# Masked multiplies, the first layer norms and the low query weights move from VectorE to GpSimd, and two weight loads trade places

## The chip, the cores and the metric

One core of one Trainium2 chip runs the whole kernel in a single launch. The metric is device time in microseconds (us) for one execution. The engines are TensorE (PE in the profile, PEld its weight loads), VectorE (DVE), ScalarE (ACT), GpSimd (POOL) and SyncE (SP), which only issues transfers here. The program is written with explicit semaphores: each engine runs its own list of instructions in order.

## The reference, cut to what matters

Two blocks of gated cross attention and feed-forward over x (8 batches of 512 tokens, width 512) with a context of 8 x 120 rows.

```python
x = x + tanh(g_xattn[0]) * L0_xattn(_layernorm(x), ctx, ctx, W_q, W_k, W_v, W_o)      # 16 heads, no mask
x = x + tanh(g_ffn[0])   * L0_ffn(_layernorm(x), ...)                                  # experts
x = x + tanh(g_xattn[1]) * L1_xattn(_layernorm(x), ctx, ctx, mask, Wq, bq, Wk, bk, Wv, bv, Wo, bo)
x = x + tanh(g_ffn[1])   * L1_ffn(_layernorm(x), W_r, W_k, W_v, mu_r, mu_k)
# in L1_xattn:
scores = jnp.where(mask == 0, -1e30, scores)     # mask: key_mask (B, 120), the same for all heads
```

Every product is taken in float32 by three passes over a high and a low part of each operand (high times high, low times high, high times low). The kernel treats the mask of layer 1 in the keys: masked columns of the context are replaced, per batch, by the mean of the columns kept.

## The kernel before

The program has a keys-and-values phase (`keys_and_values`), then attention of layer 0 (`attention(..., 0)`), the experts, attention of layer 1, and the last feed-forward. The change touches only the first phase and the hand-over to the second.

The keys-and-values phase is a list of 32 units `n`: units 0 to 7 are the keys of layer 0, 8 to 15 its values, 16 to 23 the values of layer 1, 24 to 31 its keys. Each unit is 12 matmuls (`three_passes`, L154 to L156) into one of four PSUM banks, `n % 4`; a bank is free once the unit four before it has been evicted. Evictions: keys by ACT (high part, L315) and then DVE (low part, L384 or L381); values of layer 0 by ACT (L311); values of layer 1 by DVE (L389 and L390), with a bias row that ACT makes (L304, `bvm`). SP stores each result (L214, L215, L220), and an eviction into a staging buffer waits for the store that last read it.

Each of the five engines walks through the same 32 units, and tables of `{unit: what}` say behind which unit side work stands in that engine's queue. The side work on DVE is this:

- low parts of a weight (`SPLITS`, L333), from high parts that ACT copies when the weight has landed;
- the mask tables (`MASKS`, unit 6: `held`, `dropped`, `share`), then context times `held` (`KEPT`, L394), sums by batch (`MEANS`, L398, L401), and `fill = dropped * mean`, `craw += fill` (`FILLS`, L408, L410), all on 128 x 960 tiles; at unit 23 (`RENEW`) ACT and DVE make the new high and low parts (L323, L422), which the keys of layer 1 need;
- `norm(j)` at units 1, 5, ..., 29: mean and variance of batch j of x (L355, L359, L363, L364); POOL then takes the power (L281) and SP stores it;
- `first_norm(0)` at units 16 and 18 (`NORMED`) and `first_norm(1)` at 27 and 29: the transposed x of batch 0 and 1, minus the mean and times the reciprocal deviation (L785, L788; four instructions of each for a batch); ACT then copies the high parts (`NORMED_HIGH`, for batch 1 at unit 30), DVE the low ones (`NORMED_LOW`);
- the low parts of the query weights and the expert weights at unit 21 (`query_weights_low`, L776 and L765);
- from unit 23, for the first batch of attention: low queries (L1227) and row maxima of the scores (L1234).

PE does the queries of that batch behind units 23, 24 and 26 (it waits for the low query weights at 23) and its maximum tiles behind units 24 to 31 (L1437). Behind unit 31 it transposes the maxima (L1446) and begins the scores (L1465). POOL writes constant tables behind units 0, 2, 5, 8 and 11, and takes the powers. Weights k0 and k1 share slot 2 before: k1 is loaded at unit 8, v1 early into slot 0.

Of the kernel before, what the change touches and what calls it, by code (L numbers as in the profile page):

```python
# [20 lines left out]
ALU = mybir.AluOpType  # L21
ACT = mybir.ActivationFunctionType
AX = mybir.AxisListType
# [4 lines left out]
P = 128  # L28
B, T, D = 8, 512, 512
# [19 lines left out]
def f(ap):  # L49

    return ap.bitcast(F32)
# [25 lines left out]
QUERIES_AFTER = {23: (0, 1), 24: (2,), 26: (3,)}  # L77
MAXIMA_AFTER = {n: ((n - 24) // 2, (0, 1) if n % 2 == 0 else (2, 3)) for n in range(24, 32)}
MERGE_AT, NORM_AT, QUERIES_AT, MAXIMA_AT, ROWS_AT = 39, 40, (42, 44, 47, 51), (45, 49, 53, 55), 57
Ahead = namedtuple("Ahead", "load_weights load_first load_keys load_second load_output_weight constants first_norm query_weights_high query_weights_low first_norm_high "  # L80
                            "first_norm_low begin_act begin_dve begin_pe")

Begun = namedtuple("Begun", "load_ahead gather evict_act evict_dve on_act chosen")
# [77 lines left out]
def keys_and_values(nc, sb, sem, bank, ctx_t, weights, biases, mask, mask_t, x, kh_d, kl_d, v_d, norms_d, following):  # L161
# [6 lines left out]
    raw = [sb.over(f"kv_raw{i}", [P, C, D], f"kv_wl{i}") for i in range(3)]  # L168
    ch, cl, craw = sb("kv_ch", [P, C, N], F32R), sb("kv_cl", [P, C, N], F32R), sb("kv_craw", [P, C, N])
    held, dropped = sb("kv_held", [P, N]), sb("kv_dropped", [P, N])  # L170
    fill = held
    kh, kl = sb("kv_kh", [P, NK, HALF], F32R), sb("kv_kl", [P, NK, HALF], F32R)
    vo, bvm = sb("kv_vo", [S2, NV, D + 1]), sb("kv_bvm", [S2, 2, D])
    bk, bv = sb("kv_bk", [P, C]), sb("kv_bv", [S2, D])
# [9 lines left out]
    k_hi, k_lo, v_done = sem("kv_k_hi"), sem("kv_k_lo"), sem("kv_v_done")  # L184
    k_st, v_st = [sem(f"kv_k_st{i}") for i in range(NK)], [sem(f"kv_v_st{i}") for i in range(NV)]
    mask_in, held_done, vm_done, bvm_done = sem("kv_mask_in"), sem("kv_held_done"), sem("kv_vm_done"), sem("kv_bvm_done")
    filled, new_hi, new_lo = (sem("kv_" + s) for s in ("filled", "new_hi", "new_lo"))
    x_in, norm_st = [sem(f"kv_x_in{i}") for i in range(NX)], [sem(f"kv_norm_st{i}") for i in range(3)]
    const, ve_done, rstd_done = (sem("kv_" + s) for s in ("const", "ve_done", "rstd_done"))
    chain, pchain = sem("kv_chain"), sem("kv_pchain")  # L190

    units = [(lay, kind, u) for lay, kind in ((0, "k"), (0, "v"), (1, "v"), (1, "k")) for u in range(8)]
    SLOT, TURN_OF = (2, 1, 2, 0), (0, 2, 4, 3)
    SPLITS, MASKS = {3: 1, 10: 3, 20: 2}, 6
    KEPT, MEANS, FILLS, RENEW = {7: (0, 1), 8: (2, 3)}, {9: (0, 1), 11: (2, 3)}, {12: 0, 13: 1, 14: 2, 15: 3}, 23
    NORMED, NORMED_HIGH, NORMED_LOW = {16: (0, 1), 18: (2, 3)}, {18: (0, 1), 19: (2, 3)}, {19: (0, 1), 20: (2, 3)}
    QUERY_WEIGHT, QUERY_WEIGHT_LOW = 18, 21

    def sync(sp):
        def load_w(i):  # L200
            sp.dma_start(raw[SLOT[i]][:, :, :], weights[i].rearrange("(c p) n -> p c n", p=P)).then_inc(w_in[i], 16)
# [27 lines left out]
        load_x(1)  # L229
        sp.dma_start(bk[:, :], biases[0]).then_inc(bias_in, 16)  # L230
        sp.dma_start(bv[:, :], biases[1].partition_broadcast(S2)).then_inc(bias_in, 16)
        load_w(3)
        for n, (lay, kind, u) in enumerate(units):
            if n == 8:
                for b in range(NB):
                    sp.wait_ge(full[b], 2)
                load_w(2)
            if kind == "v":
                store_v(lay, u)
            else:  # L240
                store_k(lay, u)
            if n and n % 4 == 0:
                store_norm(n // 4 - 1)
            if n % 4 == 2 and n // 4 + NX < B:
                sp.wait_ge(ve_done, n // 4 + 1)
                load_x(n // 4 + NX)
            if n == 9:
                sp.wait_ge(norm_st[0], 16)
                sp.wait_ge(held_done, 1)
                following.load_first(sp)  # L250
            if n == 12:
                following.load_weights(sp)
            if n == 17:
                for b in range(NK):
                    sp.wait_ge(k_st[b], 32 * len(range(b, 8, NK)))
                sp.wait_ge(v_st[0], 16)
                following.load_keys(sp)
            if n == 23:
                sp.wait_ge(norm_st[1], 16)
                following.load_second(sp)  # L260
# [9 lines left out]
    def gpsimd(pool):  # L270
        steps = Steps(pool, pchain)
        pool.memset(mhalf[:, :], -0.5)
        steps.link(pool.memset(vo[:, :, D:D + 1], 1.0))
        pool.drain().then_inc(const, 1)

        for n in range(len(units)):
            following.constants(pool, n)
            if n % 4 == 1:
                j = n // 4
                pool.wait_ge(ve_done, j + 1)  # L280
                pool.tensor_tensor(norms[:, j, 1, :], ve[:, :], mhalf[:, :], ALU.pow).then_inc(rstd_done, 1)  # L281

    def scalar(act):
        def high_parts(i):
# [40 lines left out]

    def vector(dve):
        steps = Steps(dve, chain)

        def low_parts(hi, lo, whole, count):

            for c in range(C):
                dve.wait_ge(hi_done, count + c + 1)
                dve.tensor_tensor(lo[:, c], whole[:, c], f(hi[:, c]), ALU.subtract).then_inc(lo_done, 1)  # L333
# [29 lines left out]
            dve.tensor_scalar(norms[:, j, 0, :], mv[:, :, 0], 1.0, None, ALU.mult)  # L363
            dve.tensor_scalar(ve[:, :], mv[:, :, 1], EPS, None, ALU.add).then_inc(ve_done, 1)  # L364

        low_parts(wh[SLOT[0]], wl[SLOT[0]], raw[SLOT[0]], 0)
        low_parts(ch, cl, craw, C)
        for n, (lay, kind, u) in enumerate(units):
            k = (8 * lay + u) % (NK if kind == "k" else NV)
# [15 lines left out]
            elif lay:  # L385
# [3 lines left out]
                dve.tensor_scalar(vo[:, k, D:D + 1], vm[:, u:u + 1], 1.0, None, ALU.mult)  # L389
                dve.scalar_tensor_tensor(out=vo[:, k, 0:D], in0=src[0:S2, :], scalar=vm[:, u:u + 1],  # L390
                                         in1=bvm[:, u % 2, :], op0=ALU.mult, op1=ALU.add).then_inc(v_done, 1)
            if n in KEPT:
                for c in KEPT[n]:
                    ins = dve.tensor_tensor(craw[:, c], craw[:, c], held[:, :], ALU.mult)  # L394
                steps.link(ins)
            if n in MEANS:
                for c in MEANS[n]:
                    ins = dve.tensor_reduce(mean[:, c], craw[:, c].rearrange("p (b s) -> p b s", s=S2), AX.X, ALU.add)  # L398
                steps.link(ins)
                of = slice(MEANS[n][0], MEANS[n][-1] + 1)  # L400
                steps.link(dve.tensor_tensor(mean[:, of], mean[:, of],  # L401
                                             share[:, :].unsqueeze(1).broadcast_to([P, len(MEANS[n]), B]), ALU.mult))
            if n in FILLS:
                c = FILLS[n]
                by_batch = lambda a: a.rearrange("p (b s) -> p b s", s=S2)
                if c:
                    dve.wait_ge(filled, c)
                steps.link(dve.tensor_tensor(by_batch(fill[:, :]), by_batch(dropped[:, :]),  # L408
                                             mean[:, c].unsqueeze(2).broadcast_to([P, B, S2]), ALU.mult))
                dve.tensor_tensor(craw[:, c], craw[:, c], fill[:, :], ALU.add).then_inc(filled, 1)  # L410
            if n in NORMED:
                following.first_norm(dve, 0, NORMED[n])
            if n in NORMED_LOW:
                following.first_norm_low(dve, 0, NORMED_LOW[n])
            if n == QUERY_WEIGHT_LOW:
                following.query_weights_low(dve)
            if n % 4 == 1:
                norm(n // 4)
            if n == RENEW:
# [91 lines left out]
def attention(nc, lay, io, early, late, sem, eight, after, front=None, turned_place=None):  # L511
# [174 lines left out]
    def constants(pool, n):  # L686
# [30 lines left out]
        if n == 11:  # L717
            steps.link(pool.memset(pick[:, :, :, :], 0.0))
            for d in range(2):
                steps.link(pool.affine_select(out=pick[:, :, :, :], in_=pick[:, :, :, :],  # L720
                                              compare_op=ALU.not_equal, fill=1.0, base=-d,
                                              pattern=[[-2, C], [-8, C], [1, DK]], channel_multiplier=0))
            pool.drain().then_inc(const, 1)
        assert steps.n == (CONST_STEPS[n][1] - (merge and n == 0) if n in CONST_STEPS else 0)

    def spread_tables(pool):
# [27 lines left out]
    def query_weights_high(act):  # L754
# [3 lines left out]
        if route:  # L758
            act.wait_ge(w_in[2], 16)
            act.activation(wch[:, :, :], raw_c[:, :, :], ACT.Copy).then_inc(e_hi, 1)  # L760

    def query_weights_low(dve):
        low_parts(dve, 0)
        dve.wait_ge(e_hi, 1)
        dve.tensor_tensor(wcl[:, :, :], raw_c[:, :, :], f(wch[:, :, :]), ALU.subtract).then_inc(e_lo, 1)  # L765

    def output_weights_high(act):
        act.wait_ge(w_in[1], 16)
# [178 lines left out]
    def gpsimd(pool):  # L947
        if merge:
            constants(pool, 0)
        else:  # L950
            low_parts(pool, 1)

        def power(count):
# [213 lines left out]
    def vector(dve, step_of=None):  # L1167
# [69 lines left out]
        def begin(dve, n):  # L1237

            if n == 22:
                steps = Steps(dve, dchain)  # L1240
                dve.wait_ge(const, 1)
                steps.link(dve.tensor_reduce(part[:, :], ident[:, :].rearrange("p (a b) -> p b a", b=2)[:, 1, :], AX.X,
                                             ALU.add))
                steps.link(dve.tensor_scalar(part[:, :], part[:, :], -1.0, None, ALU.mult))
                dve.wait_ge(c_in, 16 * 4)
                dve.wait_ge(gated, 1)
            if n in (27, 29):
                first_norm(dve, 1, (n - 27, n - 26))
            if n in MAXIMA_AFTER:
                maxima(None, *MAXIMA_AFTER[n])  # L1250
            if n in QUERIES_AFTER:
                queries(0, QUERIES_AFTER[n])
# [426 lines left out]
    if merge:  # L1679
        return Engines(sync, gpsimd, scalar, vector, tensor), banks_free, ident, mhalf, \  # L1680
            Behind(load_behind, lambda act, k: scalar(act, k), lambda dve, k: vector(dve, k),
                   lambda pe, k: tensor(pe, None, k))
    ahead = Ahead(load_weights, load_first, load_first_keys, load_second, load_output_weight, constants, first_norm, query_weights_high, query_weights_low,
                  first_norm_high, first_norm_low,
                  lambda act, n: scalar(act, n), lambda dve, n: vector(dve, n), lambda pe, n: tensor(pe, None, n))
    return Engines(sync, gpsimd, scalar, vector, tensor), ahead
# [733 lines left out]
```

## Time and profile before

| | before |
|---|---|
| median of 3 runs | 1452.23 us (1450.77 to 1454.85) |
| the profiled execution's own time | 1454.85 us |
| its span, first to last instruction | 1453.1 us |
| mean granted TensorE clock | 0.965 of full speed |
| PE busy | 1311.5 us, 90% |
| DVE busy | 907.8 us, 62% |
| ACT busy | 571.1 us, 39% |
| POOL busy | 433.1 us, 30% |

How to read it: a busy share is a mean over the whole span and the phase at hand takes a tenth of it. So tables by stretch of time are of more use. A time in the trace counts from the span's start. An instruction's duration runs from its start to its end, and the next on the same engine may start slightly before that; where several alike stand in a row, the distance of their starts is their price. In brackets behind a row is the idle time of the engine before it, and what released it.

### The profile page before, as it was taken

What the parts mean: (1) busy time and instruction counts of PE and PEld (TensorE: products, weight loads), DVE (VectorE), ACT (ScalarE), POOL (GpSimd) and SP (SyncE); (2) the same over time, 40 slices, a digit from 0 to 9 for tenths busy, and PEclk for the clock granted to TensorE, in tenths of its full rate; (3) what the DMA queues carried; (4) which work ended last, traced back from release to release, by engine and by line L of the source; (5) the groups of instructions that cost most, each with busy time, mean ns of one, the idle gap of its engine ahead of it and who ended that gap; (6) DMA issues with size and microseconds to landing.
All of it is one profiled execution on the core that took longest, in us unless ns stands there. A gap on an engine that the chain in (4) does not pass through costs nothing.

```text
span 1453.1 us, 28305 instructions
## 1 busy us (share of the span) xinstructions
PE 1311.5 (90%) x10624; PEld 938.6 (65%) x10624; DVE 907.8 (62%) x1583; ACT 571.1 (39%) x1025; POOL 433.1 (30%) x351
## 2 busy tenths in 40 slices
PE   6976899999999979886989999999996789999997
PEld 5755567777777667622436666765764677777776
DVE  6986266656666546554546655656663577777762
ACT  3331444344434445443452342343243433333331
POOL 4300335432541100000442321331130644444450
PEclk9988899999999999988999999999998899999999
DMA  9862441444233556999883552462302311111100
GB/s 330 284 181 85 165 142 65 126 165 157 78 94 122 189 169 200 339 390 368 318 333 109 173 167 77 158 201 100 125 25 88 116 44 59 59 59 59 59 32 35
DMA packets 128852, 219.55 MB, mean 151 GB/s; under 512 B 27286, under 2 KB 48278, under 8 KB 124686
## 3 DMA queue, kind: packets, MB, share of 16 engines
q1 hardware_dynamic: 128782, 218.58, 44.2%
q8 instruction: 49, 0.80, 0.2%
q14 instruction: 21, 0.17, 0.0%
HBM read 135.67 MB, written 82.88 MB: 150 GB/s over the span
## 4 chain that ended last, share of the span: by engine, by line
PE 47%; issue 22%; DVE 13%; ACT 6%; POOL 5%; DMA 5%; SPq 2%; POOLq 0%; DVEq 0%; ACTq 0%
PE b L154 8%; PE b L156 7%; PE b L155 7%; PE b L1465 3%; PE b L1919 3%; PE b L1641 3%; DVE f_mix L2134 3%; PE b L1643 2%; PE b L1642 2%; PE b L1952 2%; PE b L1437 2%; PE b L1562 2%; POOL a_atl L997 2%; PE b L1571 2%; ACT e_gt L1838 2%
## 5 line engine op out<-in xcount | busy, mean ns | idle before, releaser
L1068 ACT ACTIVATE a_pr<-b 120x512 f32<-120x512 f32 x256 | 133.9, 603 | 126.3 <-PE b L1465 126.3
L1234 DVE TENSOR_REDUCE a_mx<-b 128x4 f32<-128x480 f32 x256 | 151.9, 652 | 4.6 <-PE b L1437 4.5
L997 POOL TENSOR_TENSOR a_atl<-a_pvs,a_ath 128x512 fp32r<-128x512 f32 x64 | 81.1, 1291 | 195.6 <-ACT a_ath L1114 195.6
L956 POOL TENSOR_TENSOR a_rstd<-a_ve,a_mhalf 128x4 f32<-128x4 f32 x16 | 16.2, 1012 | 319.1 <-DVE a_ve L1183 319.1
L154 PE MATMUL b<-a_xth,a_wqh 128*128 128x512 f32 x256 | 104.0, 406 | 5.6 <-DVE a_wql L776 5.6
L1641 PE MATMUL b<-a_woh,a_ath 128*128 128x512 f32 x256 | 105.2, 411 | 2.5 <-POOL a_atl L997 2.4
L1437 PE MATMUL b<-a_kbd,a_qh 128*128 128x480 f32 x256 | 86.9, 400 | 21.1 <-DVE a_mx L1234 20.7
L1643 PE MATMUL b<-a_woh,a_atl 128*128 128x512 f32 x256 | 101.7, 397 | 0.0
L155 PE MATMUL b<-a_xtl,a_wqh 128*128 128x512 f32 x256 | 101.7, 397 | 0.0
L1642 PE MATMUL b<-a_wol,a_ath 128*128 128x512 f32 x256 | 101.6, 397 | 0.0
L156 PE MATMUL b<-a_xth,a_wql 128*128 128x512 f32 x256 | 101.6, 397 | 0.0
L1363 DVE SCALAR_TENSOR_TENSOR a_x<-b,a_gate,a_x 128x512 f32 (+1 forms) x64 | 47.8, 747 | 83.5 <-PE b L1643 83.5
L2134 DVE SCALAR_TENSOR_TENSOR f_mix<-f_dif,f_mu,f_xt 128x512 f32<-128x512 f32 x64 | 69.8, 1109 | 27.9 <-PE b L156 12.5
L1437 PEld LDWEIGHTS b<-a_kbd,a_qh 128*128 128x128 f32 x256 | 47.9, 190 | 43.6 <-DVE a_mx L1234 25.7
L1571 PE MATMUL b<-a_pr,a_vals 120*32 120x512 f32 x512 | 67.8, 600 | 0.0
L1838 ACT ACTIVATE e_gt<-b 128x512 f32<-128x512 f32 x87 | 46.1, 602 | 53.2 <-PE b L1919 53.2
L154 PEld LDWEIGHTS b<-a_xth,a_wqh 128*128 128x128 f32 x256 | 48.5, 189 | 26.2 <-issue 10.0
L2096 POOL TENSOR_TENSOR f_xmkl<-f_mix,f_xmkh 128x512 fp32r<-128x512 f32 x32 | 48.5, 1529 | 51.4 <-ACT f_xmkh L2108 51.4
L1641 PEld LDWEIGHTS b<-a_woh,a_ath 128*128 128x128 f32 x256 | 48.7, 190 | 18.3 <-issue 8.0
L1224 DVE SCALAR_TENSOR_TENSOR a_ql<-b,a_bq,a_qh 128x512 fp32r<-128x512 f32 x32 | 24.0, 751 | 56.9 <-ACT a_qh L1029 56.9
L2201 ACT ACTIVATE f_ka<-b 128x512 f32<-128x512 f32 x32 | 19.1, 597 | 98.4 <-PE b L156 92.9
L1952 PE MATMUL b<-e_gt,e_inner 32*64 32x512 f32 x384 | 51.3, 649 | 7.0 <-ACT e_xc L1856 3.3
(221 smaller groups left out, 3231.0 us busy)
## 6 DMA issues: line engine op xcount, KB each, us to landing
a_rp<-s_rp SPq DMA_DIRECT2D x128, 256.0 KB, 4.5
s_x<-a_x SPq DMA_DIRECT2D x16, 1024.0 KB, 4.2
s_rp<-e_chosen SPq DMA_DIRECT2D x16, 1024.0 KB, 7.7
s_rp<-e_xc SPq DMA_DIRECT2D x16, 1024.0 KB, 7.7
kv_xb<-in_x SPq DMA_DIRECT2D x8, 1024.0 KB, 8.3
a_xr<-in_x_t SPq DMA_DIRECT2D x8, 1024.0 KB, 6.6
a_x<-in_x SPq DMA_DIRECT2D x8, 1024.0 KB, 7.9
s_xn<-a_xn SPq DMA_DIRECT2D x8, 1024.0 KB, 4.8
```

The costliest lines, as they stand in the source:

```text
L154: pe.matmul(out, ah, bh, start=(c == 0), stop=False)
L155: pe.matmul(out, ah, bl, start=False, stop=False)
L156: last = pe.matmul(out, al, bh, start=False, stop=(c == C - 1))
L997: pool.tensor_tensor(atl[:, g], pvs[:, g], f(ath[:, g]), ALU.subtract).then_inc(a_lo, 1)
L1068: act.activation(pr[:, h % RING, :], bank[k][0:S2, :], ACT.Exp, scale=SCALE)\
L1234: dve.tensor_reduce(mx[:, t, :, r], bank[k][:, 0:HJ * S2].rearrange("p (a s) -> p a s", a=HJ), AX.X, ALU.max).then_inc(free[k], 1)
L1437: pe.matmul(bank[k][:, 0:HJ * S2], qh[:, r, t * P:(t + 1) * P], kbd[:, r, :], start=True, stop=True)\
L1571: ins = pe.matmul(bank["v"][a * DK:(a + 1) * DK, :], v[:, h * DK:(h + 1) * DK], pr[:, h % RING, :], start=True, stop=True)
L1641: pe.matmul(out, ath[:, m, cols], woh[:, m, :], start=(m == 0), stop=False)
L1642: pe.matmul(out, ath[:, m, cols], wol[:, m, :], start=False, stop=False)
L1643: ins = pe.matmul(out, atl[:, m, cols], woh[:, m, :], start=False, stop=(m == C - 1))
L2134: dve.scalar_tensor_tensor(out=mix[:, a, c % 2], in0=dif[:, c], scalar=mu[:, a, c:c + 1], in1=xt[:, c, 0:T], op0=ALU.mult, op1=ALU.add).th ...
```

## The change

- The slots of the weights: k0 and v1 now share slot 0 and k1 has slot 2. SP loads k1 early and v1 at unit 8, the other way about than before. The low parts of v1 are made at unit 11 (10 before) and those of k1 at 19 (20 before).
- Context times `held` is done by POOL, one chunk at units 9, 10, 12 and 13; a semaphore `kept` tells DVE. The means are taken chunk by chunk at units 11, 12, 14 and 15.
- The fills stand at units 16 to 19 and are, for each chunk, eight `scalar_tensor_tensor` of 120 columns (one for each batch) instead of two instructions of 960.
- `first_norm(0)` is done by POOL at units 15 and 17, behind the power of unit 17; `first_norm(1)` by POOL after unit 31's turn of its loop. The copies of the high parts stand at 18 and 20 (batch 0) and, unchanged, at 30 (batch 1).
- The low parts of the query and expert weights are made by POOL at unit 19; ACT makes the high ones at 17 (18 before).

```diff
-    SLOT, TURN_OF = (2, 1, 2, 0), (0, 2, 4, 3)
-    SPLITS, MASKS = {3: 1, 10: 3, 20: 2}, 6
-    KEPT, MEANS, FILLS, RENEW = {7: (0, 1), 8: (2, 3)}, {9: (0, 1), 11: (2, 3)}, {12: 0, 13: 1, 14: 2, 15: 3}, 23
-    NORMED, NORMED_HIGH, NORMED_LOW = {16: (0, 1), 18: (2, 3)}, {18: (0, 1), 19: (2, 3)}, {19: (0, 1), 20: (2, 3)}
-    QUERY_WEIGHT, QUERY_WEIGHT_LOW = 18, 21
+    SLOT, TURN_OF = (0, 1, 2, 0), (0, 2, 4, 3)
+    SPLITS, MASKS = {3: 1, 11: 3, 19: 2}, 6
+    KEPT, MEANS, FILLS, RENEW = {9: 0, 10: 1, 12: 2, 13: 3}, {11: 0, 12: 1, 14: 2, 15: 3}, {16: 0, 17: 1, 18: 2, 19: 3}, 23
+    NORMED, NORMED_HIGH, NORMED_LOW = {15: (0, 1), 17: (2, 3)}, {18: (0, 1), 20: (2, 3)}, {20: (0, 1), 21: (2, 3)}
+    QUERY_WEIGHT = 17
...
-        load_w(3)
+        load_w(2)
         for n, (lay, kind, u) in enumerate(units):
             if n == 8:
                 for b in range(NB):
                     sp.wait_ge(full[b], 2)
-                load_w(2)
+                load_w(3)
...
         for n in range(len(units)):                      # gpsimd
             following.constants(pool, n)
+            if n in KEPT:
+                c = KEPT[n]
+                pool.wait_ge(held_done, 1)
+                pool.wait_ge(lo_done, C + c + 1)
+                pool.tensor_tensor(craw[:, c], craw[:, c], held[:, :], ALU.mult).then_inc(kept, 1)
             if n % 4 == 1:
                 j = n // 4
                 pool.wait_ge(ve_done, j + 1)
                 pool.tensor_tensor(norms[:, j, 1, :], ve[:, :], mhalf[:, :], ALU.pow).then_inc(rstd_done, 1)
+            if n in NORMED:
+                following.first_norm(pool, 0, NORMED[n])
...
             if n in MEANS:                               # vector
-                for c in MEANS[n]:
-                    ins = dve.tensor_reduce(mean[:, c], craw[:, c].rearrange("p (b s) -> p b s", s=S2), AX.X, ALU.add)
...
+                c = MEANS[n]
+                dve.wait_ge(kept, c + 1)
+                steps.link(dve.tensor_reduce(mean[:, c], craw[:, c].rearrange("p (b s) -> p b s", s=S2), AX.X, ALU.add))
+                steps.link(dve.tensor_tensor(mean[:, c], mean[:, c], share[:, :], ALU.mult))
             if n in FILLS:
                 c = FILLS[n]
-                steps.link(dve.tensor_tensor(by_batch(fill[:, :]), by_batch(dropped[:, :]),
-                                             mean[:, c].unsqueeze(2).broadcast_to([P, B, S2]), ALU.mult))
-                dve.tensor_tensor(craw[:, c], craw[:, c], fill[:, :], ALU.add).then_inc(filled, 1)
-            if n in NORMED:
-                following.first_norm(dve, 0, NORMED[n])
+                for b in range(B):
+                    ins = dve.scalar_tensor_tensor(out=craw[:, c, of_batch(b)], in0=dropped[:, of_batch(b)],
+                                                   scalar=mean[:, c, b:b + 1], in1=craw[:, c, of_batch(b)],
+                                                   op0=ALU.mult, op1=ALU.add)
+                ins.then_inc(filled, 1)
...
+        if route and n == 19:                            # constants(pool, n)
+            for c in range(C):
+                pool.wait_ge(w_hi[0], c + 1)
+                pool.tensor_tensor(wql[:, c], raw_q[:, c], f(wqh[:, c]), ALU.subtract).then_inc(w_lo[0], 1)
+            pool.wait_ge(e_hi, 1)
+            pool.tensor_tensor(wcl[:, :, :], raw_c[:, :, :], f(wch[:, :, :]), ALU.subtract).then_inc(e_lo, 1)
...
         else:                                            # attention's gpsimd, ahead of its first turn
+            first_norm(pool, 1, range(C))
             low_parts(pool, 1)
...
-            if n in (27, 29):                            # attention's begin(dve, n)
-                first_norm(dve, 1, (n - 27, n - 26))
```

## Rows read from the trace of the kernel before

**Rows 1.** The head of the profile's page.

```profile
span 1453.1 us, 28305 instructions
PE 1311.5 (90%) x10624; PEld 938.6 (65%) x10624; DVE 907.8 (62%) x1583; ACT 571.1 (39%) x1025; POOL 433.1 (30%) x351
```

**Rows 2.** Stretches: busy time (instructions) of each engine, granted clock, DMA share, GB/s.

```profile
40.00:60.00 20.00, 20.00 (x88) 15.63 (x87) 19.60 (x32) 5.49 (x10) 6.99 (x7) 1.00 1.02 323
60.00:80.00 20.00, 17.08 (x66) 12.76 (x65) 19.74 (x40) 7.18 (x12) 2.86 (x2) 0.91 0.76 231
80.00:100.00 20.00, 12.72 (x47) 9.21 (x46) 19.76 (x43) 10.89 (x17) 1.01 (x1) 0.83 0.54 142
```

**Rows 3.** PE in order of time (start, duration), and one stretch of 5 us.

```profile
91.01 0.80 PE L154 MATMUL b<-a_xth,a_wqh 128*128 128x512 f32 x1 [5.59 <-DVE a_wql L776]
...
125.46 0.77 PE L1437 MATMUL b<-a_kbd,a_qh 128*128 128x480 f32 x1 [3.12 <-DVE a_mx L1234]
...
139.36 1.33 PE L1437 MATMUL b<-a_kbd,a_qh 128*128 128x480 f32 x2 [6.08 <-DVE a_mx L1234]
...
125.00:130.00 5.00, 4.54 (x14) 3.70 (x15) 2.73 (x5) 0.00 (x0) 0.00 (x0) 0.66 0.28 99
```

**Rows 4.** DVE's groups, 0 to 150 us: busy us, mean ns | idle before.

```profile
L785 DVE TENSOR_TENSOR a_xr<-a_xr,a_mr 128x512 f32<-128x512 f32 x8 | 8.9, 1147 | 0.0
L788 DVE TENSOR_TENSOR a_xr<-a_xr,a_mr 128x512 f32<-128x512 f32 x8 | 8.6, 1109 | 0.0
...
L394 DVE TENSOR_TENSOR kv_craw<-kv_craw,kv_held 128x960 f32<-128x960 f32 x4 | 5.5, 1421 | 0.0
...
L408 DVE TENSOR_TENSOR kv_held<-kv_dropped,kv_mean 128x960 f32<-128x960 f32 x4 | 4.6, 1156 | 0.1
...
L422 DVE TENSOR_TENSOR kv_cl<-kv_craw,kv_ch 128x960 fp32r<-128x960 f32 x4 | 4.4, 1152 | 0.0
...
L776 DVE TENSOR_TENSOR a_wql<-a_raw_q,a_wqh 128x512 fp32r<-128x512 f32 x4 | 2.5, 689 | 0.0
```

**Rows 5.** POOL in order of time, and one of its groups over the whole span.

```profile
134.85 1.78 POOL L281 TENSOR_TENSOR kv_norms<-kv_ve,kv_mhalf 128x4 f32<-128x4 f32 x1 [21.53 <-DVE kv_ve L364]
163.29 4.98 POOL L776 TENSOR_TENSOR a_wol<-a_raw_o,a_woh 128x512 fp32r<-128x512 f32 x4 [26.67 <-ACT a_woh L770]
...
178.09 2.54 POOL L997 TENSOR_TENSOR a_atl<-a_pvs,a_ath 128x512 fp32r<-128x512 f32 x2 [0.57 <-ACT a_ath L1114]
180.58 6.45 POOL L785 TENSOR_TENSOR a_xr<-a_xr,a_mr 128x512 f32<-128x512 f32 x4
...
L968 POOL TENSOR_TENSOR a_sums<-a_pick,a_vals 120x512 f32<-120x512 f32 x8 | 8.3, 1040 | 18.2 <-DMA a_vals<-s_v 18.2
```

**Rows 6.** DVE and POOL in order of time while both run, 37 to 44 us.

```profile
37.68 0.62 POOL L713 TENSOR_SCALAR_AFFINE_SELECT a_xr<-a_xr 128x480 f32<-128x480 f32 x1
39.17 1.15 DVE L394 TENSOR_TENSOR kv_craw<-kv_craw,kv_held 128x960 f32<-128x960 f32 x1
39.20 1.59 POOL L713 TENSOR_SCALAR_AFFINE_SELECT a_xr<-a_xr 128x480 f32<-128x480 f32 x1
40.24 1.56 DVE L394 TENSOR_TENSOR kv_craw<-kv_craw,kv_held 128x960 f32<-128x960 f32 x1
40.93 1.33 POOL L713 TENSOR_SCALAR_AFFINE_SELECT a_xr<-a_xr 128x480 f32<-128x480 f32 x1
41.83 1.44 DVE L394 TENSOR_TENSOR kv_craw<-kv_craw,kv_held 128x960 f32<-128x960 f32 x1
42.33 1.39 POOL L715 CAST a_mpick<-a_xr 128x480 fp32r<-128x480 f32 x1
```

**Rows 7.** Line 1338 by itself (ns min/median/max), and both engines near its longest.

```profile
L1338 DVE SCALAR_TENSOR_TENSOR a_rx<-a_rx,a_part,a_rs x16: 350/350/1273, 169.7 to 1130.8; 128x128 fp32r<-128x128 f32 x16
...
1130.78 1.27 DVE L1338 SCALAR_TENSOR_TENSOR a_rx<-a_rx,a_part,a_rs 128x128 fp32r<-128x128 f32 x1
...
1128.86 3.04 POOL L2096 TENSOR_TENSOR f_xmkl<-f_mix,f_xmkh 128x512 fp32r<-128x512 f32 x2 [1.29 <-ACT f_xmkh L2108]
```

**Rows 8.** The load issued at 41.63 (last number: us to landing), and ACT's eviction of unit 15.

```profile
kv_raw<-in_k SPq DMA_DIRECT2D x1, 1024.0 KB, 8.5
...
63.05 0.60 ACT L311 ACTIVATE kv_vo<-b 120x512 f32<-120x512 f32 x1 [3.40 <-DMA s_v<-kv_vo]
```

**Rows 9.** DVE and PE in order of time: the last norm and the phase's end.

```profile
131.61 0.69 DVE L355 BATCH_NORM_STATS2 kv_stats<-kv_xb 128x6 f32<-128x512 f32 x1
...
134.61 0.16 DVE L364 TENSOR_SCALAR kv_ve<-kv_mv 128x4 f32<-128x4 f32 x1
...
148.32 0.63 PE L1446 MATMUL b<-a_ident,a_mx 128*128 128x128 f32 x4 [2.33 <-DVE a_mx L1234]
```

More of the change, by code:

```diff
@@ L79 @@
 MERGE_AT, NORM_AT, QUERIES_AT, MAXIMA_AT, ROWS_AT = 39, 40, (42, 44, 47, 51), (45, 49, 53, 55), 57
-Ahead = namedtuple("Ahead", "load_weights load_first load_keys load_second load_output_weight constants first_norm query_weights_high query_weights_low first_norm_high "
+Ahead = namedtuple("Ahead", "load_weights load_first load_keys load_second load_output_weight constants first_norm query_weights_high first_norm_high "
                             "first_norm_low begin_act begin_dve begin_pe")
@@ L170, in keys_and_values @@
     held, dropped = sb("kv_held", [P, N]), sb("kv_dropped", [P, N])
-    fill = held
     kh, kl = sb("kv_kh", [P, NK, HALF], F32R), sb("kv_kl", [P, NK, HALF], F32R)
@@ L186, in keys_and_values @@
     mask_in, held_done, vm_done, bvm_done = sem("kv_mask_in"), sem("kv_held_done"), sem("kv_vm_done"), sem("kv_bvm_done")
-    filled, new_hi, new_lo = (sem("kv_" + s) for s in ("filled", "new_hi", "new_lo"))
+    kept, filled, new_hi, new_lo = (sem("kv_" + s) for s in ("kept", "filled", "new_hi", "new_lo"))
     x_in, norm_st = [sem(f"kv_x_in{i}") for i in range(NX)], [sem(f"kv_norm_st{i}") for i in range(3)]
@@ L327, in vector @@
         steps = Steps(dve, chain)
+        of_batch = lambda b: slice(b * S2, (b + 1) * S2)
         def low_parts(hi, lo, whole, count):
@@ L364, in norm @@
             dve.tensor_scalar(ve[:, :], mv[:, :, 1], EPS, None, ALU.add).then_inc(ve_done, 1)
-        low_parts(wh[SLOT[0]], wl[SLOT[0]], raw[SLOT[0]], 0)
+        low_parts(wh[0], wl[0], raw[0], 0)
         low_parts(ch, cl, craw, C)
@@ L391, in vector @@
                                          in1=bvm[:, u % 2, :], op0=ALU.mult, op1=ALU.add).then_inc(v_done, 1)
[L392 to L395, printed above, removed]
             if n in MEANS:
-                for c in MEANS[n]:
-                    ins = dve.tensor_reduce(mean[:, c], craw[:, c].rearrange("p (b s) -> p b s", s=S2), AX.X, ALU.add)
[L399 to L402, printed above, removed]
+                c = MEANS[n]
+                dve.wait_ge(kept, c + 1)
+                steps.link(dve.tensor_reduce(mean[:, c], craw[:, c].rearrange("p (b s) -> p b s", s=S2), AX.X, ALU.add))
+                steps.link(dve.tensor_tensor(mean[:, c], mean[:, c], share[:, :], ALU.mult))
             if n in FILLS:
                 c = FILLS[n]
-                by_batch = lambda a: a.rearrange("p (b s) -> p b s", s=S2)
-                if c:
-                    dve.wait_ge(filled, c)
-                steps.link(dve.tensor_tensor(by_batch(fill[:, :]), by_batch(dropped[:, :]),
-                                             mean[:, c].unsqueeze(2).broadcast_to([P, B, S2]), ALU.mult))
-                dve.tensor_tensor(craw[:, c], craw[:, c], fill[:, :], ALU.add).then_inc(filled, 1)
-            if n in NORMED:
-                following.first_norm(dve, 0, NORMED[n])
+                for b in range(B):
[3 more added lines that the diff above has]
+                ins.then_inc(filled, 1)
             if n in NORMED_LOW:
                 following.first_norm_low(dve, 0, NORMED_LOW[n])
-            if n == QUERY_WEIGHT_LOW:
-                following.query_weights_low(dve)
             if n % 4 == 1:
@@ L760, in query_weights_high @@
             act.activation(wch[:, :, :], raw_c[:, :, :], ACT.Copy).then_inc(e_hi, 1)
[L762 to L765, printed above, removed]
     def output_weights_high(act):
@@ L1682, in attention @@
                    lambda pe, k: tensor(pe, None, k))
-    ahead = Ahead(load_weights, load_first, load_first_keys, load_second, load_output_weight, constants, first_norm, query_weights_high, query_weights_low,
+    ahead = Ahead(load_weights, load_first, load_first_keys, load_second, load_output_weight, constants, first_norm, query_weights_high,
                   first_norm_high, first_norm_low,
```

## The prediction

> **What bounds the kernel now.** I read the page's head first [rows 1], then the table of stretches [rows 2]. The diff reorders only the first tenth, the keys-and-values phase, so that is the place to look. From 40 to 100 us VectorE (DVE) is busy 19.6 to 19.8 of every 20 us while TensorE (PE) falls from 20.0 to 12.7: DVE sets the pace. After 100 us neither is full and they wait for each other. The reader sees this in PE's own rows [rows 3]: before the first query matmul it sat idle 5.59 us for the low weights that DVE writes; at 125.46 and 139.36 it waited 3.12 and 6.08 us for row maxima that stood in DVE's queue behind first_norm. The phase ends where PE turns the maxima, at 148.32; everything later hangs on that point.
>
> **The change: what leaves DVE.** Durations are from [rows 4] (a group's busy time). Between DVE's first masking multiply (39.17) and the end of its RENEW low parts (100.9, the 4.4 us group of L422) leave: the four masking multiplies 5.5; half of L785 and L788 (batch 0), 8.75; the low query weights 2.5 plus one more of that width, 0.6. The fills were 4.6 (L408) and as much again (L410), 9.2. They become 32 multiply-adds of 120 columns. No such row exists; 960 and 512 columns cost 1.09 and 0.62 each, so the slope gives 0.2 for 120; I take 0.18, 32 are 5.8, saving 3.4. (Bounds: 0.13 by columns alone, 0.35 by the lone 128-column row [rows 7].) Two more mean multiplies add 0.3. Sum taken off: 5.5 + 8.75 + 3.1 + 3.4 - 0.3 = 20.5.
>
> **What GpSimd (POOL) pays.** By [rows 5] first_norm costs 1.61 per instruction (6.45 for 4), a low part 1.25 to 1.27, a pow 1.0 undisturbed (1.78 at worst). A 960-column multiply isn't there: from 1.27 by columns 2.35; bounds 1.95 to 3.0 (from the plain 1.04 of a 512-column product elsewhere and from 1.61).
>
> **The two engines block each other.** The masking stretch shows it [rows 6]: POOL's L713 takes 0.62 alone, but 1.59 and 1.33 while DVE's two-input multiplies run, and DVE's 1.15 becomes 1.56 and 1.44. They take turns, one whole instruction each: DVE 40.24 can't read until POOL's ends, POOL's 40.93 until DVE's ends at 41.80, and DVE's 41.83 again waits. It hits small instructions hardest [rows 7]: a 128-column L1338 normally takes 0.35 and took 1.27, ending just after POOL's L2096. The Trainium skill (SBUF — State Buffer, Who interferes with whom) says the same in its own terms: a DVE instruction with two SBUF inputs and a GpSimd one that reads SBUF exclude each other for the whole instruction; the trace agrees, and this rule speaks against the change. Evictions from PSUM and bn_stats have at most one SBUF input; in 180 to 193 us POOL's rate stays 1.61 beside them.
>
> **Waits that come in, followed instruction by instruction.**
> 1. v1's weight is now the one loaded late, at unit 8, and needed at unit 11. Its predecessor in that place of the queue (issued 41.63) took 8.5 us [rows 8], so it lands at 50.1; ScalarE (ACT) copies until 50.8. DVE gets there at 39.2 + 3.1 for the norm [rows 9] = 42.3. POOL starts masking at 41.1 (43.7 in the trace, less 2.6 it lost to L394), and is at its third product until 51.65: mask, pow, mask, 2.4 of constants, mask. DVE waits 9.35.
> 2. The second low part waits for the fourth mask: 2.35.
> 3. Then two means, the norm until 62.1, pow until 63.1 and first_norm's first four. Two mean multiplies wait for it: 1.9. The eviction of unit 16 isn't the bound: it could begin once ACT has evicted unit 15 at 63.05, which waits for a store [rows 8].
> 4. Unit 16's fills meet the last two of those four: 0.9 + 1.6 = 2.5.
> 5. Unit 17's norm ends at 76.6 and releases POOL just as DVE goes into unit 18. POOL now has a pow, four first_norm and five low parts in a row. Each of the eight fills waits for one: 0.35 + 4 x 1.61 + 3 x 1.25 = 10.5. They end at 89.2.
> 6. The last two POOL low parts hold up k1's: 2.5.
>
> Sum 29.1. DVE ends RENEW 29.1 - 20.5 = 8.6 later, at 109.5. PE follows: unit 23 needs the eviction of unit 19, queued behind all of 5 and 6, at about 95, so the earlier weights (about 90) don't help it.
>
> **After RENEW.** Batch 1's first_norm leaves DVE. PE's wait of 3.12 and some slow clock after it go: in 125 to 130 us the granted clock is 0.66 [rows 3], that is 1.7 us. I take 4.8 in all, up to the last norm. The second half no longer matters to PE alone, since POOL runs all eight after that norm, ACT waits for them at unit 30, and unit 31's keys are behind it in ACT's queue. Before, from 134.77 to 148.32 took 13.55 [rows 9]. Now: pow 1.0 + 8 x 1.61 = 12.9 + ACT's last copy 0.63 and eviction 0.66 + DVE 0.72 and maxima 1.22 + hand-overs 0.4 = 17.5. That is +3.9. PE, DVE and SP's next loads wait with it; the output weights of the next turn follow on POOL but are not due for 15 us. The earlier k1 load and the turned inputs land well ahead and cost nothing; if v1's landed 3 us later, all would be 3 later.
>
> Total: +8.6 - 4.8 + 3.9 = +7.7. The profiled execution took 1454.85, 2.6 above the median of 1452.2; the difference applies to either, so I forecast 1452.2 + 7.7 = 1459.9, about 1460.
>
> **Rivals.**
> - *Relief wins (faster).* The small fills slip past POOL, several or all between two of its instructions, because a 0.13 us read may find the port free. Then waits 3 to 6 (17.4) go; PE is bound by POOL's low query weights at about 84.5 instead. Queries end at 91.7 and unit 24 at 94.4 against 102.1: -7.7, then -4.8 + 3.9: -8.6, 1443.6. For it: no row has several tiny DVE instructions against a POOL run. Against: [rows 6, 7]. It decides when the six waits together fall under 21.6.
> - *It cancels.* A few fills pass per gap, so wait 5 is 3.5 rather than 10.5: +0.7, 1453. For: the gaps of POOL are unknown; against: in [rows 6] DVE's next instruction never got in ahead of a waiting POOL.
> - *The early stretch hurts more.* Masks of 3.0: +2.6, and v1 landing later: 1463. [Rows 5] speak for the smaller figure.
>
> **Chances.** Forecast with its own spread (masks 1.95 to 3.0: -1.5 to +2.6; fills clear of POOL: -0.8 to +2.6; clock 1 either way) 1456.5 to 1464: 0.55, and the heavier early stretch 0.1. Relief 0.18, cancelling 0.17. No change means within 0.3%, 4.4 us, about what this kernel's measurement can tell. The forecast lies 3.3 beyond that bound; of its 0.65, 0.05 falls inside. So slower 0.6, same 0.22, faster 0.18. The likeliest case's range is 1456.5 to 1464; as both signs are alive, the range given is 1444 to 1464.
>
> **What the next profile will show.** Right: DVE idle from about 42 to 51 in front of wl; the new 120-column fills, of which eight lie about 1.3 to 1.8 apart around 78 to 89; PE with one gap of over 10 us before unit 23; ACT waiting for POOL's mult before unit 31's keys; PE's transposed maxima near 156. Wrong: fills evenly 0.2 apart beside a busy POOL (then faster); v1's weight landing before 46; POOL's first_norm over 2 us apiece; the transposed maxima under 145.

## The result

| | before | changed |
|---|---|---|
| median | 1453.14 us (1450.77 to 1454.85, 4 runs) | 1462.16 us (1461.76 to 1464.07, 4 runs) |
| span of the profiled execution | 1453.1 us | 1461.7 us |

Changed over before is 1.0065, 95% interval 1.0048 to 1.0084: slower by 9.0 us (7 to 12). 1460 had been forecast, in a range of 1444 to 1464 (from a base of 1452.2, the median before a fourth run of before had joined).

First the head of the profile's page after the change. DVE is busy only 7 us less than before [rows 1] and POOL 37 us more.

```profile
PE 1308.4 (90%) x10624; PEld 937.8 (64%) x10624; DVE 900.5 (62%) x1584; ACT 571.1 (39%) x1025; POOL 470.0 (32%) x376
```

The stretches, against [rows 2]. From 40 to 60 us DVE is down from 19.60 to 12.83, but that is no relief: 6.95 us of it are idling before v1's low parts (the next block), and what left its list there is made up by waits. From 80 to 100 us it is busy all 20.00, while PE has fallen from 12.72 to 8.76 and the granted clock from 0.83 to 0.63. A DVE instruction that waits for POOL counts as busy, as the next blocks show.

```profile
40.00:60.00 20.00, 20.00 (x88) 15.66 (x87) 12.83 (x21) 5.56 (x10) 13.49 (x10) 1.00 1.02 321
60.00:80.00 20.00, 15.37 (x62) 11.41 (x62) 19.71 (x51) 9.61 (x17) 10.17 (x7) 0.94 0.82 245
80.00:100.00 20.00, 8.76 (x27) 6.41 (x27) 20.00 (x30) 4.29 (x7) 11.84 (x9) 0.63 0.34 88
```

DVE in order of time, changed kernel (start, duration; in brackets the idle time before). The first row is v1's low parts, late behind the weight; then the same eight 120-column fills (L407) at four units; L340 at 87.31 is k1's low parts.

```profile
50.75 5.56 DVE L340 TENSOR_TENSOR kv_wl<-kv_raw,kv_wh 128x512 fp32r<-128x512 f32 x4 [6.95 <-ACT kv_wh L293]
...
67.38 4.21 DVE L407 SCALAR_TENSOR_TENSOR kv_craw<-kv_dropped,kv_mean,kv_craw 128x120 f32<-128x120 f32 x8
...
72.24 2.10 DVE L407 SCALAR_TENSOR_TENSOR kv_craw<-kv_dropped,kv_mean,kv_craw 128x120 f32<-128x120 f32 x8
...
78.07 9.32 DVE L407 SCALAR_TENSOR_TENSOR kv_craw<-kv_dropped,kv_mean,kv_craw 128x120 f32<-128x120 f32 x8
87.31 5.68 DVE L340 TENSOR_TENSOR kv_wl<-kv_raw,kv_wh 128x512 fp32r<-128x512 f32 x4
...
104.64 4.36 DVE L418 TENSOR_TENSOR kv_cl<-kv_craw,kv_ch 128x960 fp32r<-128x960 f32 x4
```

The last row is RENEW's low parts, which end at 109.0. In the kernel before they ended at 100.9:

```profile
96.53 4.36 DVE L422 TENSOR_TENSOR kv_cl<-kv_craw,kv_ch 128x960 fp32r<-128x960 f32 x4
```

The same eight fills take 2.10, 4.21 or 9.32 us. What POOL does at those times explains it: nothing at 72.24, the last two of a run of four at 67.38, and at 78.07 the beginning of a run of nine.

```profile
63.23 3.36 POOL L782 TENSOR_TENSOR a_xr<-a_xr,a_mr 128x512 f32<-128x512 f32 x2
66.56 3.37 POOL L785 TENSOR_TENSOR a_xr<-a_xr,a_mr 128x512 f32<-128x512 f32 x2
77.52 1.01 POOL L285 TENSOR_TENSOR kv_norms<-kv_ve,kv_mhalf 128x4 f32<-128x4 f32 x1 [7.59 <-DVE kv_ve L371]
78.49 3.11 POOL L782 TENSOR_TENSOR a_xr<-a_xr,a_mr 128x512 f32<-128x512 f32 x2
81.56 3.16 POOL L785 TENSOR_TENSOR a_xr<-a_xr,a_mr 128x512 f32<-128x512 f32 x2
84.69 5.49 POOL L723 TENSOR_TENSOR a_wql<-a_raw_q,a_wqh 128x512 fp32r<-128x512 f32 x4
90.14 1.71 POOL L725 TENSOR_TENSOR a_wcl<-a_raw_c,a_wch 128x512 fp32r<-128x512 f32 x1
```

And PE, the rows that answer to [rows 3] and the last of [rows 9]: one wait of 11.24 us before unit 23, and one of 11.72 at the end. Of the two waits for maxima in between, the one of 3.12 is gone and the one of 6.08 has shrunk to 2.11 (at 140.19).

```profile
93.86 0.75 PE L154 MATMUL b<-kv_wh,kv_ch 128*120 128x512 f32 x1 [11.24 <-DVE kv_vo L397]
...
156.03 1.09 PE L1442 MATMUL b<-a_ident,a_mx 128*128 128x128 f32 x4 [11.72 <-DVE a_mx L1232]
```

The transposed maxima come at 156.03 instead of 148.32, 7.7 later. The reader can find that gap in the chain of work that ended last: the last norm's power, then eight POOL instructions, then ACT's eviction of unit 31. PE's own last work ends at 144.31, and from there on it is idle.

```profile
139.66 1.01 POOL kv_norms L285
140.66 6.10 POOL a_xr L782 x4
146.77 5.91 POOL a_xr L785 x4
152.72 0.51 issue
153.23 0.65 ACT kv_kh L321
```

### The profile page after: what moved, and what is told of

Its sections match the earlier page's. It is cut to its first block, busy times and chain, and to the rows that moved or that the text cites. A ratio compares the mean times of both kernels' runs of the same rounds, so it can differ in the third digit from the quotient of the medians.

```text
span 1461.7 us, 28338 instructions
## 1 busy us (share of the span) xinstructions
PE 1308.4 (90%) x10624; PEld 937.8 (64%) x10624; DVE 900.5 (62%) x1584; ACT 571.1 (39%) x1025; POOL 470.0 (32%) x376
## 4 chain that ended last, share of the span: by engine, by line
PE 48%; issue 22%; DVE 12%; ACT 6%; POOL 5%; DMA 4%; SPq 1%; POOLq 0%; DVEq 0%; ACTq 0%
PE b L154 8%; PE b L156 8%; PE b L155 7%; PE b L1461 3%; PE b L1637 3%; PE b L1638 3%; PE b L1639 3%; PE b L1915 2%; DVE f_mix L2130 2%; PE b L1948 2%; PE b L1558 2%; PE b L1433 2%; ACT a_pr L1066 2%; POOL a_atl L995 2%; PE b L1567 2%
## 5 line engine op out<-in xcount | busy, mean ns | idle before, releaser
L1637 PE MATMUL b<-a_woh,a_ath 128*128 128x512 f32 x256 | 106.2, 415 | 3.6 <-POOL a_atl L995 3.6
L1637 PEld LDWEIGHTS b<-a_woh,a_ath 128*128 128x128 f32 x256 | 49.1, 192 | 19.2 <-issue 9.2
L1639 PEld LDWEIGHTS b<-a_woh,a_atl 128*128 128x128 f32 x256 | 49.4, 193 | 11.9
```

Of the source, the lines that this page charges most:

```text
L1637: pe.matmul(out, ath[:, m, cols], woh[:, m, :], start=(m == 0), stop=False)
L1639: ins = pe.matmul(out, atl[:, m, cols], woh[:, m, :], start=False, stop=(m == C - 1))
```

## The experiments

The yardstick beside the median is the start of the transposed maxima: 148.32 before, 156.03 changed. It comes from one profile each. It shows where in the phase a difference arises, which a median can't (single executions of before ran from 1448.98 to 1458.16 us; its medians beside the experiments were 1453.8, 1453.7 and 1454.1).

The mark carries the TensorE clock of that one execution, and this part can be read off. With first_norm(1) gone from DVE, PE waits for maxima twice, 2.11 us each (120.96 and 140.19 in the changed kernel), and runs the same matmuls between. From the end of one wait to the end of the other it takes 17.7 us in four profiles (wide fills, low parts back, first_norm(0) back, before with first_norm(1) at unit 25) and 19.2 in the five others, where one stretch of 5 us after the first wait was granted only 0.66 to 0.77. So 1.5 us between two marks can be the clock alone. What decides it isn't shown: the wait ahead of it is 2.11 or 2.12 us in all nine.

**Is work on POOL free for DVE?** Two kernels add useless work on POOL to the kernel before, once with reads, once without, on a spare tile that nothing else uses.

```diff
+    spare = sb("kv_spare", [P, D])                   # and a memset of it once, at the start
...
                 pool.tensor_tensor(norms[:, j, 1, :], ve[:, :], mhalf[:, :], ALU.pow).then_inc(rstd_done, 1)
+            if n == 17:
+                for _ in range(10):                   # second kernel: range(24)
+                    steps.link(pool.tensor_tensor(spare[:, :], spare[:, :], spare[:, :], ALU.mult))
+                                                      # second kernel: pool.memset(spare[:, :], 0.0)
```

> The kernel before, with ten more 512-column multiplies on POOL, both inputs and the output in a spare tile, right after the power of unit 17, about 77 to 90 us. They compute nothing that is used. Theory A: DVE, with two-input work in that stretch, waits for most of them, up to 1.27 us each: RENEW ends 7 to 12 us later, time 6 to 12 more. Rival (engines run beside each other freely): below 1 us.

> The kernel before, with 24 memsets of the same spare tile on POOL instead, 0.5 us each, so the same 12 us of POOL time at the same place without a read. Theory A (the two exclude each other only where POOL reads SBUF): within 1 us of the kernel before. If any POOL work slowed DVE: as much as with the multiplies.

With the multiplies: 1460.30 us, ratio 1.0052 (1.0036 to 1.0069), maxima at 154.31. With the memsets: 1455.22 us, 1.0015 (1.0005 to 1.0025), maxima at 148.72. k1's low parts (four of DVE's) and POOL beside them, first with the multiplies:

```profile
77.14 17.96 POOL L286 TENSOR_TENSOR kv_spare<-kv_spare 128x512 f32<-128x512 f32 x10
...
84.00 5.86 DVE L338 TENSOR_TENSOR kv_wl<-kv_raw,kv_wh 128x512 fp32r<-128x512 f32 x4
```

then with the memsets:

```profile
77.21 13.95 POOL L286 MEMSET kv_spare<- 128x512 f32 x24
...
83.01 2.49 DVE L338 TENSOR_TENSOR kv_wl<-kv_raw,kv_wh 128x512 fp32r<-128x512 f32 x4
```

5.86 against 2.49 for the same four. 14 us of POOL writes leave DVE's durations as they were. Beside POOL's multiplies seven of DVE's two-input instructions lost 0.84 us each and three more about 0.1; DVE had been 0.4 ahead, and RENEW ended 5.9 later, just under the 7 to 12 that I had expected. The 1.5 us that the memsets seem to cost is a little over the 1 us expected, and its interval (1.0005 to 1.0025) lies above 1. RENEW isn't later there (it begins at 96.13, before at 96.53), so up to there it doesn't come of DVE waiting; where it comes from isn't shown. So the price lies in the pairing of reads. The Trainium skill (SBUF — State Buffer, Who interferes with whom) makes just this distinction between a GpSimd instruction that reads SBUF and one that only writes; both runs agree.

**Is it the eight small fills?**

```diff
-                for b in range(B):
-                    ins = dve.scalar_tensor_tensor(out=craw[:, c, of_batch(b)], in0=dropped[:, of_batch(b)], ...)
-                ins.then_inc(filled, 1)
+                steps.link(dve.tensor_tensor(by_batch(held[:, :]), by_batch(dropped[:, :]), mean[:, c]..., ALU.mult))
+                dve.tensor_tensor(craw[:, c], craw[:, c], held[:, :], ALU.add).then_inc(filled, 1)
```

> The changed kernel with each fill as two 960-column instructions again (4 x 2 instead of 4 x 8). Theory A: the sum of both engines' work in the stretch counts, not the size of the pieces. Fills cost 9.3 instead of 8.3 by themselves, POOL's nine instructions stay: RENEW's low parts end within 2 us of 109.0, time within 2 us of the changed kernel's. Rival C (eight small fills, each behind one long POOL instruction, are the loss): two waits instead of six in unit 18, 5 us earlier or more.

1463.82 us, 1.0071 (1.0049 to 1.0092): no gain. RENEW ends at 108.0 against 109.0, and this execution was already 0.9 ahead at v1's low parts. (The maxima stand at 154.17, 1.9 earlier; 1.5 of that is the clock, this being one of the four profiles with 17.7.) The waits moved on to what follows:

```profile
79.15 2.54 DVE L411 TENSOR_TENSOR kv_craw<-kv_craw,kv_held 128x960 f32<-128x960 f32 x1
81.61 7.52 DVE L340 TENSOR_TENSOR kv_wl<-kv_raw,kv_wh 128x512 fp32r<-128x512 f32 x4
```

The fills end at 81.7 instead of 87.4, and k1's low parts take 7.52 instead of 5.68, then the next fills wait as well. As long as DVE's queue holds such work, it goes at POOL's pace, mostly one instruction of DVE's for each of POOL's, whichever instructions do the waiting. A turn lasts about as long as POOL's instruction, with DVE's own time inside it: in unit 18 a fill takes 1.59 to 1.68 us beside POOL's 1.56 to 1.64, and 1.34 beside 1.30. The rival of the small pieces falls.

**Is it the late load of v1?**

```diff
-    SLOT, TURN_OF = (0, 1, 2, 0), (0, 2, 4, 3)
+    SLOT, TURN_OF = (2, 1, 2, 0), (0, 2, 4, 3)        # v1 loaded early, k1 at unit 8, as before
```

> The changed kernel with the slots and the two weight loads back as before (v1 loaded early, k1 at unit 8), all else changed. Theory A (DVE and POOL take turns on two-input work, and the tail waits for POOL): the 7 us that DVE stands idle before v1's low parts go, but unit 16's eviction can't be earlier than about 64.6, when ACT has evicted unit 15 and made the bias row, and it stands at 66.7 now; so the transposed maxima come 1 to 3 us earlier than at 155.9. Rival B (the late load is the loss): 7 to 9 us earlier.

1463.20 us, 1.0065 (1.0049 to 1.0082), maxima at 154.75, 1.3 earlier. The 6.95 us of idling at 50.75 are gone, and most of them come back further on:

```profile
43.70 4.57 DVE L340 TENSOR_TENSOR kv_wl<-kv_raw,kv_wh 128x512 fp32r<-128x512 f32 x4
...
65.25 0.15 DVE L396 TENSOR_SCALAR kv_vo<-kv_vm 120x1 f32<-120x1 f32 x1 [6.03 <-ACT kv_bvm L310]
```

Unit 16's eviction waits for ACT, and ACT for a store of values (63.90 here, 63.05 in [rows 8]). So the late load is worth 1.4 us, not the 9 that DVE loses there.

**Which of the moved work pays?** Two kernels give part of it back to DVE.

```diff
+            if n == 21:                                # vector; taken from POOL's unit 19
+                following.query_weights_low(dve)
```

> The changed kernel with the five low parts of the query and expert weights on DVE at unit 21 again. Theory A: POOL's run behind unit 17 shrinks from nine to four instructions, 6.5 us less for DVE to wait, 3.1 more for it to do: RENEW ends 3 to 4 us earlier, time 3.4 less than the changed kernel's. If work on POOL were free for DVE, it would be 3 us later instead.

```diff
-            if n in NORMED:                            # gpsimd, NORMED = {15: (0, 1), 17: (2, 3)}
-                following.first_norm(pool, 0, NORMED[n])
+            if n in NORMED:                            # vector, NORMED = {16: (0, 1), 18: (2, 3)}
+                following.first_norm(dve, 0, NORMED[n])
```

> The changed kernel with first_norm(0) on DVE at units 16 and 18 again. Theory A: DVE has 8.75 us more to do, and loses about 10 us of waits (two mean multiplies 1.8, two fills 2.3, four fills 6.2); the five low parts of POOL at unit 19 still meet DVE's two-input work. RENEW ends between 3 us earlier and 1 us later. If POOL's work were free for DVE: 8 us later.

Low parts back: RENEW ends at 106.2 (2.8 earlier with 3.1 more work on DVE), maxima at 151.66, 4.4 earlier, of which 1.5 is the clock; 1461.28 us, 1.0055 (1.0038 to 1.0072), which the median alone doesn't tell from the changed kernel (3.4 less had been expected). first_norm(0) back: 8.3 us more work on DVE by its rows, and RENEW ends at 108.3, 0.7 earlier; maxima at 153.76, 2.3 earlier, again 1.5 of it the clock; 1463.31 us, 1.0069 (1.0052 to 1.0086). With the low parts back, POOL's run ends at 84.2 and k1's low parts are at their own price again:

```profile
77.42 7.44 DVE L407 SCALAR_TENSOR_TENSOR kv_craw<-kv_dropped,kv_mean,kv_craw 128x120 f32<-128x120 f32 x8
84.78 2.48 DVE L340 TENSOR_TENSOR kv_wl<-kv_raw,kv_wh 128x512 fp32r<-128x512 f32 x4
```

Neither move to POOL had relieved DVE: each costs it as much in waits as in work, or more.

**The tail.** First the changed kernel, then the kernel before, each with first_norm(1) at unit 25 of POOL's loop; then the kernel before with it where the change puts it.

```diff
+            if n == 25:                                # gpsimd, behind the power of unit 25
+                following.first_norm(pool, 1, range(C))
...
-            first_norm(pool, 1, range(C))              # ahead of attention's first turn (or DVE's units 27 and 29)
```

> The changed kernel with first_norm(1) on POOL right after the power of unit 25 instead of after unit 31's turn of its loop. Theory A: it lies at about 121 to 134, beside DVE work with at most one SBUF input, so it costs nothing; ACT evicts unit 31 when PE is done with it, near 142 instead of 153.2, and the transposed maxima come 9 to 12 us earlier, about 145.5; time about 1451.5. Rival D (the tail is not on the path; PE would be late anyway): under 3 us.

> The kernel before, with first_norm(1) alone moved to POOL, right after the power of unit 25. It stands beside DVE work with at most one SBUF input. Theory A: PE's waits of 3.12 and 6.08 us shrink by 3.1 and 4.0 and its clock has no such pauses to fall in; the transposed maxima come 8 to 11 us earlier than at 148.3; time 1442 to 1445. Rival (another wait takes over, such as ACT waiting for POOL at unit 30): under 4 us gained.

> The kernel before with first_norm(1) alone moved to POOL, after unit 31's turn of its loop as in the changed kernel. It puts the prediction's two last terms by themselves: -4.8 up to the last norm (its ve at about 130 instead of 134.6), +3.9 from there to the transposed maxima. Theory A: the maxima at 147.5, 0.9 earlier than before, so no change in time (within 2 us). Against the run with it at unit 25, whose maxima stand at 138.54, the same work is 9 us later for its place in POOL's queue alone.

| first_norm(1) | maxima at | median | over before |
|---|---|---|---|
| changed, after the loop | 156.03 | 1462.16 | 1.0065 (1.0048 to 1.0084) |
| changed, at unit 25 | 147.03 | 1452.20 | 0.9992 (0.9980 to 1.0004) |
| before + POOL after the loop | 148.11 | 1454.97 | 1.0009 (0.9995 to 1.0022) |
| before + POOL at unit 25 | 138.54 | 1443.46 | 0.9933 (0.9917 to 0.9950) |

The marks of the last three rows of the table, as the profiles have them:

```profile
147.03 0.63 PE L1443 MATMUL b<-a_ident,a_mx 128*128 128x128 f32 x4 [2.40 <-DVE a_mx L1233]
148.11 1.08 PE L1445 MATMUL b<-a_ident,a_mx 128*128 128x128 f32 x4 [11.79 <-DVE a_mx L1235]
138.54 0.93 PE L1446 MATMUL b<-a_ident,a_mx 128*128 128x128 f32 x4 [2.40 <-DVE a_mx L1236]
```

The same eight instructions, at a place where DVE has no work with two SBUF inputs and nobody yet waits, are worth 9.0 and 9.6 us of the mark (of the 9.6 the clock gave 1.5; the first pair has the same clock). That is twice: the whole loss of the change in one case, and a kernel 10 us faster than before in the other. Of the last kernel, POOL, then ACT:

```profile
113.22 6.51 POOL L787 TENSOR_TENSOR a_xr<-a_xr,a_mr 128x512 f32<-128x512 f32 x4
119.69 6.45 POOL L790 TENSOR_TENSOR a_xr<-a_xr,a_mr 128x512 f32<-128x512 f32 x4
129.95 1.01 POOL L281 TENSOR_TENSOR kv_norms<-kv_ve,kv_mhalf 128x4 f32<-128x4 f32 x1 [3.81 <-DVE kv_ve L366]
...
128.97 2.17 ACT L795 ACTIVATE a_xth<-a_xr 128x512 fp32r<-128x512 f32 x4
135.75 0.66 ACT L317 ACTIVATE kv_kh<-b,kv_bk 128x480 fp32r<-128x480 f32 x1 [4.60 <-PE b L156]
```

ACT's copies need no wait and its eviction of unit 31 waits for PE alone.

**A version with the masks as well**, on the best one: masks on POOL at units 9, 10, 12 and 13, small fills at 12 to 15.

```diff
-    KEPT, MEANS, FILLS = {7: (0, 1), 8: (2, 3)}, {9: (0, 1), 11: (2, 3)}, {12: 0, 13: 1, 14: 2, 15: 3}
+    KEPT, MEANS, FILLS = {9: 0, 10: 1, 12: 2, 13: 3}, {12: 0, 13: 1, 14: 2, 15: 3}, {12: 0, 13: 1, 14: 2, 15: 3}
```

> The kernel before with first_norm(1) on POOL at unit 25, and in addition the masking multiplies on POOL (units 9, 10, 12, 13) and small fills in place of wide ones, at units 12 to 15 as before, so that they end before anything else is on POOL. DVE saves 5.5 + 1; it can't evict unit 16 before about 64.6 (ACT evicts unit 15 at 63.05 and makes the bias row), against 67.6, so at most 3 us come of it; the low parts of v1 meet the masks and lose up to 2 each. Theory A: maxima at 135.5 to 138.5, time 1440.5 to 1443.5. If the masks' turns with DVE cost more than they save: later than 138.5.

Maxima at 141.51, 3.0 later than without the masks on POOL; 1444.36 us, 0.9936 (0.9913 to 0.9959), so the median sees no difference. I had expected 135.5 to 138.5. Half of the 3.0 is the clock (19.2 here, 17.7 there), the other half was there at the end of RENEW (102.4 against 100.8): the fills are dearer than I had them, and the first eight met two masks.

```profile
49.99 6.16 DVE L407 SCALAR_TENSOR_TENSOR kv_craw<-kv_dropped,kv_mean,kv_craw 128x120 f32<-128x120 f32 x8
```

## Why the prediction was right, step by step

- **DVE sets the pace up to RENEW; relief must be counted net of waits.** Right. RENEW ended at 109.0 (forecast 109.5) against 100.9.
- **What leaves DVE, 20.5.** Too high by 2.4 for the fills. Eight of them alone take 2.10 us, 0.26 each from start to start, not 0.18. The slope between wide instructions had given 0.2, and I had gone below it without a reason; 0.26 lies inside my bounds (0.13 to 0.35).
- **Wait 1, 9.35.** v1 landed 8.5 us after its issue, ACT was done as forecast: 6.95 of idling, 1.5 for the norm's L370 behind a mask (1.66 instead of 0.17; the prediction had that instruction free) and 1.0 in the first low part: 9.4. But its worth was only 1.4, as the run with the early load shows; about 2 us separated it from the next bound, ACT's eviction of unit 15, which the prediction named without drawing that conclusion.
- **Waits 2 to 4, 2.35, 1.9 and 2.5.** 2.1, 1.8 (L403 took 1.74 and 0.41 instead of 0.17) and 2.1.
- **Waits 5 and 6, 10.5 and 2.5.** 7.2 (9.32 less 2.10) and 3.2 (5.68 less 2.49). The turns are as foreseen, one fill for one POOL instruction, but two fills slipped by while POOL took the power, so the fills met six POOL instructions and not seven (1.6 with the power's rest). And a turn lasts as long as POOL's instruction with the fill's 0.26 inside, where I had added the two (another 1.6). Wait 5 was too long by 3.3, and that cancels the error of the fills: two wrong terms of opposite sign stand behind the good 8.6 (8.1 measured). That closeness is luck.
- **-4.8 up to the last norm.** 3.3: from RENEW's end the norm came 30.6 us later, before 33.9. PE's wait behind first_norm is gone, but the clock fell elsewhere, to the lower of its two levels (1.2 instead of 2.4 GHz) for part of a stretch: 120 to 125 us was granted 0.71 (first row), where before the same matmuls had 1.00 in 112 to 117 (second row). The term itself was right for a profile without that fall: in the kernel before the last norm came 4.9 earlier with first_norm(1) at unit 25 (17.7 us between the waits), and 3.15 earlier with it after the loop (19.2).

```profile
120.00:125.00 5.00, 3.96 (x10) 2.96 (x11) 3.19 (x9) 0.00 (x0) 1.01 (x1) 0.71 0.27 99
```

```profile
112.00:117.00 5.00, 4.07 (x17) 3.13 (x18) 3.11 (x7) 0.27 (x1) 1.01 (x1) 1.00 0.27 100
```

- **+3.9 in the tail.** 2.9: 16.45 us from the last norm to the maxima, before 13.55. POOL's eight took 12.1, not 12.9 (1.5 each).
- **Sum +7.7.** 8.1 - 3.3 + 2.9 = 7.7 at the maxima. But 1.5 of it is the clock of the one profiled execution, which no term held; without that fall it would be 6.2, so the exact match is chance. The medians differ by 9.0, the spans by 8.6. Up to 210 us the delay stays at 7.8 (POOL's next power begins at 209.53, before at 201.74); where the last us arises I haven't shown, and it is within the interval.
- **The rivals.** "Relief wins" needed small fills that pass POOL; the only two that did so stood beside a power. "It cancels" needed a gain of 7 in wait 5; it was 3.3. "The early stretch hurts more" needed masks of 3.0 or a later v1; the first took 2.26, and v1 came as forecast.

## What to carry to other kernels

Before moving elementwise work from VectorE to GpSimd, list what VectorE will be running at that moment. Against work with two SBUF inputs VectorE falls to GpSimd's slower pace, and in this case the move gained nothing. Against evictions from PSUM, reductions and the statistics instructions it was free, and 10 us were to be had that way here. And look who stands behind the new instruction: placed behind the last norm it kept ScalarE idle for 12 us, and the last eviction came 9 us later (153.23 instead of 144.24 with it at unit 25). A stall of 9 us may be worth 1.4 if another bound stands 2 us behind it.

## What I had not expected of the hardware

- "Two inputs" is not the whole of it. The norm's L370 has one input, 128 x 4 values, and took 1.66 us instead of 0.17 beside the first mask on POOL, which ran from 41.44 to 43.70 (1.67 in the kernel with v1 early, too). In the kernel before, L341 with 128 x 8 took 0.97 beside a POOL cast. Which small instructions wait isn't shown.

```profile
42.07 1.66 DVE L370 TENSOR_SCALAR kv_norms<-kv_mv 128x4 f32<-128x4 f32 x1
```

- GpSimd's power on 128 x 4 values (L285) takes 1.01 us but didn't hold up the two fills beside it, at 0.33 and 0.34 us each.
- The turns aren't always one for one. In the kernel with useless multiplies POOL's first, issued at 77.14, had to wait until four of DVE's strided 512-column instructions in a row were through. They ran at their usual price, and it took 4.95 us instead of 1.37:

```profile
77.14 4.95 POOL L286 TENSOR_TENSOR kv_spare<-kv_spare 128x512 f32<-128x512 f32 x1
...
78.93 1.20 DVE L793 TENSOR_TENSOR a_xr<-a_xr,a_mr 128x512 f32<-128x512 f32 x1
```

Why DVE kept its turn there and not between its plain subtractions stays open; no run here varies the strides.
